# Two graph-attention layers on one core: the same steps in another order on every engine

## The chip, the cores and the metric

The kernel runs on one core of a Trainium2 chip. The metric is the device time of one execution in microseconds (us): the median of three runs before the change is 1123.22 us, the runs lie between 1122.74 and 1124.8. All views below come from one profiled execution of the kernel before.

## The reference

64 graphs of 128 nodes with 384 features pass two attention layers; every layer is followed by a residual and a layer norm. Cut to what is computed:

```python
# layer 0: 6 heads of 64
q, k, v = heads(x @ Wq + bq), heads(x @ Wk + bk), heads(x @ Wv + bv)
probs = softmax(q @ k.T / 8 + where(adj, 0, -9e15))
x1 = layernorm(x + (probs @ v) @ Wf + bf)
# layer 1: 12 heads of 32
h = x1 @ W                                   # per head
src, dst = tanh(h) . w_src, tanh(h) . w_dst
attn = leaky_relu(src + dst.T, 0.2); attn[~adj] = -999; attn = softmax(attn)
feat = elu(attn @ h + b)
gate = sigmoid(x1 @ H_w.T + H_b)
out = layernorm(x1 + gate * feat + (1 - gate) * x1)
```

## The kernel before, in words

The work goes pair by pair: 32 pairs of graphs, and g (0 or 1) is the graph in its pair. Large products are made of three passes in a high and a low part (`product`, L454 to L461): nine matmuls of 384 columns for a 128x384 result, two times nine of 256 columns for the queries and keys of one third j of the heads.

All five engines run one loop over turns (`turns`, L108 to L120). Each engine has its own list of steps, written out by hand at the end of its block, and works it off in this order: an engine that waits in one step does not go on to the next. What a step waits for are counters of other steps (`now` and `prev`, L71 to L75). A step is given the stage of its pair: in turn t, `turn.step(0, ...)` works on pair t, `turn.step(1, ...)` on pair t-1; `turn.late` works one pair further back, so that `late(0, ...)` is on pair t-1 and `late(2, ...)` on pair t-3. The first turns, -1 to 3, and the last ones, 31 to 34, are written out; a step whose pair does not exist is left out in them.

One pair's way, with the names used below (PE is TensorE, DVE VectorE, ACT ScalarE, POOL GpSimd, SP the engine that issues DMAs):

- qk0, qk1, qk2 (PE `queries_keys`, L479): queries and keys in PSUM; ACT copies them as q_hi and k_hi (L721, L722), DVE subtracts to q_lo and k_lo (L964, L967). sc0 and sc1 (`scores`, L545) need all three j of them. v0, v1 are the values.
- DVE adds the mask and takes the minimum, ACT takes the exponent, PE transposes the weights (pt00, pt01, pt10, pt11: graph and half, L567), att0 multiplies them by the values, ct transposes the context, pr projects it, and x1 is normed (`norm0`, ACT L813).
- Layer 1: PE transposes x1 (x1t0, x1t1, L498), h0 and h1 (`hidden`) and the gate's rows g0, g1 multiply it. ACT takes tanh (th), POOL multiplies (prod, L1318), DVE sums (L1008) and splits the sums in three small parts, PE transposes these (sdt, L529), ACT copies them to sd_t (L765), a DMA lays them flat, and PE makes the logits z0, z1 (`attention1`, L613 and L617).
- z goes ACT copy (L793), DVE leak (`z_leak`, L1129), DVE maximum (`z_maxima`, L1136), POOL subtract (`z_subtract`, L1353), ACT exponent (L818). Then a third is transposed by PE (wt0, wt1, L626) and the rest by DMA, out of p_hi (ACT L824) and p_lo (`weights1_low`, POOL L1360). a1, written attend1(g, k), multiplies the weights by h in three parts of 12 matmuls (L640, L642); features, gate, mix, norm1 (ACT L840) and the store follow.

PSUM has two banks for the large products (lin), two for transposes (tp), three joined ones for scores and logits (zp) and one for the two attentions (fp). `LIN_USERS`, `TP_USERS`, `ZP_USERS` and `FP_USERS` (L124 to L127) list who uses them, in PE's order; `SECOND_BANK` says which users take the second bank, and `last_reader` (L140) finds from these lists whose reader PE has to wait for.

## Time and profile before

| | |
|---|---|
| median of three runs | 1123.22 us |
| span of the profiled execution | 1121.2 us, 2.0 below the median |
| PE busy, weight loads | 1047.1 us (93%), 950.8 us (85%) |
| DVE, ACT, POOL busy | 1025.2 (91%), 893.5 (80%), 947.2 us (84%) |
| DMA | 91.33 MB, mean 81 GB/s |
| one turn in the middle | 32.65 us |

The span is cut by the pipeline: the first four turns fill it, turns 4 to 30 repeat the same pattern to a hundredth of a microsecond, and from turn 31 on it drains. PE's matmuls are pipelined, so the start of a row less the start of the row before it is what one matmul costs; the length in a row is longer. A wait of PE can stand on PE or on its weight loads (PEld).

### The profile page before, as it was taken

How to read it: one execution, taken by the hardware profiler on the slowest of the kernel's cores; microseconds unless marked ns; L12 is line 12 of the kernel's file. 1: busy time of each engine (PE TensorE's matmuls, PEld its weight loads, DVE VectorE, ACT ScalarE, POOL GpSimd, SP SyncE). 2: the span in 40 equal slices, each digit the busy share in tenths (PEclk: the TensorE clock that was granted, in tenths of full speed). 3: DMA queues.
4: the chain of work that ended last, by engine and by line, in shares of the span. 5: the costliest groups of instructions: out<-in, count | busy, mean ns of one | idle time of the engine just before them, and what ended most of it. 6: DMA issues, size and time to landing. Idle time of an engine off the chain costs nothing.

```text
span 1121.2 us, 32794 instructions
## 1 busy us (share of the span) xinstructions
PE 1047.1 (93%) x10890; PEld 950.8 (85%) x10890; DVE 1025.2 (91%) x2138; ACT 893.5 (80%) x1739; POOL 947.2 (84%) x781
## 2 busy tenths in 40 slices
PE   4899999999999999999999999999999999999761
PEld 4888889889898988889898888889888888988641
DVE  5589999999999999999999999999999999999854
ACT  4568888888888888888888888888888888888753
POOL 2158889988888998888899888889988888998775
PEclk9899999999999999999999999999999999999975
DMA  6103333232333333234333323433332243332232
GB/s 200 32 21 73 98 84 89 76 86 66 82 97 83 89 79 84 70 79 97 83 89 81 82 74 74 97 83 89 83 82 77 69 97 83 93 81 72 47 67 73
DMA packets 188717, 91.33 MB, mean 81 GB/s; under 512 B 158864, under 2 KB 183696, under 8 KB 188688
## 3 DMA queue, kind: packets, MB, share of 16 engines
q1 hardware_dynamic: 188688, 90.95, 32.7%
q8 instruction: 17, 0.28, 0.1%
q14 instruction: 12, 0.10, 0.0%
HBM read 31.61 MB, written 12.58 MB: 39 GB/s over the span
## 4 chain that ended last, share of the span: by engine, by line
PE 73%; issue 9%; DVE 8%; POOL 4%; ACT 3%; DMA 1%; DVEq 0%; SPq 0%; POOLq 0%; ACTq 0%
PE lin L459 42%; PE zp L554 6%; PE zp L613 3%; PE zp L617 3%; PE fp L583 3%; PE tp L498 3%; PE tp L567 3%; PE tp L626 2%; DVE sd L1008 2%; PE tp L595 2%; PE fp L586 2%; PE fp L640 2%; ACT th L736 1%; ACT sd_t L765 1%; POOL z L1353 1%
## 5 line engine op out<-in xcount | busy, mean ns | idle before, releaser
L1353 POOL TENSOR_TENSOR z<-z,z_max 128x1536 f32<-128x1536 f32 x64 | 176.4, 2757 | 21.3 <-DVE z_max L1136 18.9
L818 ACT ACTIVATE z<-z,log_scale 128x1536 f32<-128x1536 f32 x64 | 101.3, 1583 | 53.7 <-POOL z L1353 53.6
L1360 POOL TENSOR_TENSOR p_lo<-z,p_hi 128x1024 f16<-128x1024 f32 x64 | 137.3, 2145 | 2.3 <-ACT p_hi L824 2.3
L1365 POOL TENSOR_TENSOR f<-f,x_kept 128x384 f32<-128x384 f32 x64 | 65.0, 1016 | 72.0 <-DVE f L1168 72.0
L1318 POOL TENSOR_TENSOR prod<-th,w_sd_rows 128x768 f32<-128x768 f32 x64 | 117.9, 1842 | 6.6 <-ACT th L736 6.4
L784 ACT ACTIVATE p<-p,p_min 128x128 f32<-128x128 f32 x384 | 118.9, 399 | 4.7 <-DVE p_min L1068 4.7
L1129 DVE SCALAR_TENSOR_TENSOR z<-zp,z 128x1536 f32<-128x1536 f32 x64 | 111.9, 1748 | 2.3 <-ACT z L793 2.3
L1136 DVE TENSOR_REDUCE z_max<-z 128x12 f32<-128x1536 f32 x64 | 111.6, 1744 | 0.1
L793 ACT ACTIVATE z<-zp 128x1536 f32<-128x1536 f32 x64 | 93.2, 1457 | 17.8 <-PE zp L617 17.8
L1331 POOL TENSOR_TENSOR v_part<-v_res,v_part 128x384 bf16<-128x384 f32 x64 | 63.0, 984 | 35.8 <-ACT v_part L755 33.8
L459 PE MATMUL lin<-xt_hi,Wq_hi 128*128 128x256 f32 x288 | 81.0, 281 | 12.7 <-DVE Wk_lo L926 12.4
L640 PE MATMUL fp<-h_part,p1t_hi 128*128 128x33 f16 x1536 | 71.9, 178 | 9.5 <-DMA p1t_lo<-p_lo 6.9
L459 PE MATMUL lin<-xt_lo,Wq_hi 128*128 128x256 f32 x288 | 80.5, 280 | 0.0
L459 PE MATMUL lin<-xt_hi,Wq_lo 128*128 128x256 f32 x288 | 80.5, 280 | 0.0
L459 PE MATMUL lin<-xt_hi,Wk_lo 128*128 128x256 f32 x288 | 80.4, 279 | 0.0
L459 PE MATMUL lin<-xt_hi,Wk_hi 128*128 128x256 f32 x288 | 80.4, 279 | 0.0
L459 PE MATMUL lin<-xt_lo,Wk_hi 128*128 128x256 f32 x288 | 80.4, 279 | 0.0
L1378 POOL TENSOR_TENSOR y<-f,x_kept 128x384 f32<-128x384 f32 x64 | 70.3, 1098 | 7.6 <-ACT out_tile L840 7.2
L640 PEld LDWEIGHTS fp<-h_part,p1t_hi 128*128 128x128 f16 x1536 | 63.6, 96 | 14.2 <-DMA p1t_lo<-p_lo 7.3
L1076 DVE SCALAR_TENSOR_TENSOR p0t_lo<-tp,p0t_hi 128x384 f16<-128x384 f32 x128 | 67.1, 545 | 7.5 <-ACT p0t_hi L799 4.5
L459 PE MATMUL lin<-Hw_hi,x1t_hi 128*128 128x384 f32 x192 | 73.8, 384 | 0.0
L459 PE MATMUL lin<-W_hi,x1t_hi 128*128 128x384 f32 x192 | 71.1, 371 | 2.1 <-DVE x1t_lo L975 2.0
(162 smaller groups left out, 4394.2 us busy)
## 6 DMA issues: line engine op xcount, KB each, us to landing
xt_raw<-x_t SPq DMA_DIRECT2D x32, 384.0 KB, 4.0
...
dst_row<-sd_t SPq DMA_DIRECT2D x64, 9.0 KB
p1t_hi<-p_hi SPq DMA_TRANSPOSE x64, 3.2
p1t_lo<-p_lo SPq DMA_TRANSPOSE x64, 3.1
```

Of the source, the lines that this page charges most:

```text
L459: last = pe.matmul(bank, a(k), b(k), start=(opens and k == 0 and i == 0), stop=(k == C - 1 and i == 2))
L554: last = pe.matmul(zp[:, half, N * j:N * (j + 1)], q[p, j, own], k[p, j, own], start=(j == 0 and i == 0), stop=(i == 2), skip_group_check= ...
L640: pe.matmul(o, hi, h_part[i][:, g, h, :], start=(h == 0 and i == 0), stop=False, skip_group_check=True)
L784: last = act.activation(p0[:, g, N * h:N * (h + 1)], p0[:, g, N * h:N * (h + 1)], ACT.Exp, bias=p0_min[:, g, h:h + 1], scale=-1.0)
L793: act.activation(z[:, g, :], zp[:, :, :].rearrange("p b n -> p (b n)"), ACT.Copy)\
L818: act.activation(z[:, g, :], z[:, g, :], ACT.Exp, bias=log_scale[:, :]).then_inc(z_exp[g].sem, 1)
L1129: dve.scalar_tensor_tensor(out=z[:, g, :], in0=zp[:, :, :].rearrange("p b n -> p (b n)"), scalar=0.2, in1=z[:, g, :], op0=ALU.mult, op1=AL ...
L1136: dve.tensor_reduce(z_max[:, g, :], z[:, g, :].rearrange("p (a n) -> p a n", a=H1), AX.X, ALU.max).then_inc(z_maxed[g].sem, 1)
L1318: pool.tensor_tensor(prod[:, g, :].rearrange("p (s d) -> p s d", s=2), th[:, g:g + 1, :].to_broadcast([128, 2, D]), rows["w_sd"][:, :].rea ...
L1353: pool.tensor_tensor(zs, zs, z_max[:, g, :].unsqueeze(2).to_broadcast([128, H1, N]), ALU.subtract)\
L1360: pool.tensor_tensor(p1_lo[:, g, :], z[:, g, PE_HEADS * N:], p1_hi[:, g, :], ALU.subtract).then_inc(w1_lo[g].sem, 1)
L1378: pool.tensor_tensor(y2[:, g, :], f[:, g, :], x1_kept[:, g, :], ALU.add).then_inc(y2_ready[g].sem, 1)
```

## The change

Nothing is computed in another way. Each engine's list has another order; the four lists of PSUM users follow PE's new order, and `SECOND_BANK` becomes a table with other members. A new `later` works two pairs further back, and some steps change from `step` to `late` or from `late` to `later` (or back), which moves them across the border of the turn. Turns -1 to 4 are now written out, and the loop begins at turn 5. On SP two waits that stood together are separated by the loop's spare increment.

```diff
+    def shifted(self, turns, stage, function, *which):
+
+        if self.runs(stage, turns):
+            self.behind = turns
             function(*which)
             self.behind = 0
...
+    def late(self, stage, function, *which):
+        self.shifted(1, stage, function, *which)
+
+    def later(self, stage, function, *which):
+        self.shifted(2, stage, function, *which)
...
-    for t in range(-1, 4):
+    for t in range(-1, 5):
...
-    with eng.Fori(4, PAIRS - 1) as t:
+    with eng.Fori(5, PAIRS - 1) as t:
...
-LIN_USERS = ("h1", "g0", "qk0", "v0", "pr0", "g1", "pr1", "qk1", "qk2", "v1", "h0")
+LIN_USERS = ("qk1", "h0", "qk2", "qk0", "h1", "v0", "v1", "pr0", "g0", "g1", "pr1")
...
-        turns_back += users[i] in LATE_USERS
+        turns_back += LATE_USERS.get(users[i], 0)
...
                     sp.wait_ge(w1_hi[g].sem, now(w1_hi[g]))
+                    turn.apart()
                     sp.wait_ge(f_mm[g].sem, now(f_mm[g]))
...
-                turn.late(0, scores, 1)
+                turn.step(0, scores, 1)
...
-                turn.step(1, hidden, 0)
+                turn.late(1, hidden, 0)
```

PE's turn was x1t1, sc1, a1(0), h1, pt00, pt01, g0, qk0, a1(1) with sdt inside it, pt10, pt11, att0 0, z0, ct0, att0 1, v0, pr0, ct1, z1, g1, pr1, qk1, qk2, wt0, x1t0, v1, sc0, h0, wt1. It is now qk1, h0, att0 0, pt10, qk2, wt0, qk0, pt11, x1t1, a1(0) with sc0 inside it, h1, ct0, wt1, v0, sc1, a1(1) with v1 inside it, pr0, sdt, att0 1, pt00, g0, ct1, z0, g1, pr1, pt01, x1t0, z1.

First place: PE ahead of sc0. Before, from the last matmul of qk2 (lin1) through wt0, x1t0 and the nine matmuls of v1 (lin0) to the first of sc0 (zp); qk_lo0 to qk_lo2 are DVE's counters for q_lo and k_lo:

```order
L459 MATMUL lin1<-xt_hi,Wk_lo 128x256
L626 MATMUL tp1<-ident,z 128x128 [waits ct_lo,z_exp]
L626 MATMUL tp1<-ident,z 128x128 x3
L498 MATMUL tp0<-ident,x1 128x128 [waits pt_lo0,x1_ready]
L498 MATMUL tp0<-ident,x1 128x128 x2
L459 MATMUL lin0<-Wv_hi,xt_hi 128x384 [waits xt_split,qk_lo1]
...
L554 MATMUL zp<-k_hi,q_hi 128x128 [waits qk_lo1,qk_lo2,qk_lo0,z_leaky]
```

Now, from the last matmul of qk0 (lin0) through pt11, x1t1 and twelve matmuls of a1 to sc0:

```order
L470 MATMUL lin0<-xt_hi,Wk_lo 128x256
L578 MATMUL tp1<-ident,p0 128x128 [waits wt_lo,sc_exp]
L578 MATMUL tp1<-ident,p0 128x128 x2
L509 MATMUL tp0<-ident,x1 128x128 [waits pt_lo0,x1_ready]
L509 MATMUL tp0<-ident,x1 128x128 x2
L651 MATMUL fp<-h_part0,p1t_hi 128x33 [waits wt_lo,h_done1,ctx_ready]
...
L565 MATMUL zp<-k_hi,q_hi 128x128 [waits qk_lo1,qk_lo2,qk_lo0,z_leaky]
```

The last product that sc0 needs now stands two times three transposes and twelve small matmuls ahead of it, without a large product in between.

Second place: PE around sdt. Before, in the last part of a1(1); the counters sd_part3 (DVE's small parts) and sd_copied (ACT's sd_t) are those of the same turn:

```order
L642 MATMUL fp<-h_part0,p1t_lo 128x33
L529 MATMUL tp0<-ident_bf,sd_parts 128x128 [waits pt_lo0,sd_part3]
L529 MATMUL tp0<-ident_bf,sd_parts 128x128
L640 MATMUL fp<-h_part0,p1t_hi 128x33
...
L567 MATMUL tp0<-ident,p0 128x128 [waits sd_copied,sc_exp]
L567 MATMUL tp0<-ident,p0 128x128 x2
```

Now, from the last matmul of pr0 (lin1) through sdt and att0 1 (fp from v_part and p0t) to pt00:

```order
L470 MATMUL lin1<-Wf_hi,ctx_lo 128x384
L540 MATMUL tp1<-ident_bf,sd_parts 128x128 [waits wt_lo,sd_part3]
L540 MATMUL tp1<-ident_bf,sd_parts 128x128
L594 MATMUL fp<-v_part0,p0t_hi 128x65 [waits pt_lo0,v_done2,f_norm]
...
L578 MATMUL tp1<-ident,p0 128x128 [waits sd_copied,sc_exp]
L578 MATMUL tp1<-ident,p0 128x128 x2
```

sdt moved behind pr0, and 30 matmuls of att0 instead of 12 of a1 stand between it and the transposes that wait for its reader.

Third place: POOL around the two z_subtract (z, z_max). Before, both stood in the middle of the turn, with a step of the values, the mix, a deviation and the mask between them:

```order
L1353 TENSOR_TENSOR z<-z,z_max 128x1536 [waits z_maxed]
L1330 ISA
L1331 TENSOR_TENSOR v_part2<-v_res,v_part1 128x6x64 [waits v_done1]
L1378 TENSOR_TENSOR y2<-f,x1_kept 128x384 [waits out_ready,x1_copied1,f_gated]
L1343 ISA
L1344 TENSOR_TENSOR rstd<-rstd,half_neg 128x1 [waits y_var]
L1290 REGISTER_ALU
L1294 TENSOR_SCALAR mask0<-adj0 128x256 [waits adj0_loaded,sc_masked]
L1353 TENSOR_TENSOR z<-z,z_max 128x1536 [waits z_maxed]
```

Now graph 0's is the last step of a turn, and graph 1's stands in the next turn between the two `weights1_low` (p1_lo):

```order
L1371 TENSOR_TENSOR p1_lo<-z,p1_hi 128x1024 [waits wt_turned0]
L1364 TENSOR_TENSOR z<-z,z_max 128x1536 [waits z_maxed]
L1326 REGISTER_ALU
L1329 TENSOR_TENSOR prod<-th,w_sd_rows 128x768 [waits sd_sum,h_tanh]
L1309 REGISTER_ALU
L1313 TENSOR_SCALAR mask1<-adj1 128x256 [waits adj1_loaded,z_mm]
L1371 TENSOR_TENSOR p1_lo<-z,p1_hi 128x1024 [waits wt_turned1,w1_hi]
L1329 TENSOR_TENSOR prod<-th,w_sd_rows 128x768 [waits sd_sum,h_tanh]
```

What follows z on every engine moved with it: exponent, p_hi, p_lo, wt, a1, the features, norm1 and the store of a pair are now all in the turn after the one of its z0 and z1. A pair's first step, qk1, is the first of PE's turn t, and its last, norm1 of graph 1, the last of ACT's turn t+3.

## Rows read from the trace of the kernel before

**Rows 1.** Page, busy time of each engine, share of span, instructions

```profile
PE 1047.1 (93%) x10890; PEld 950.8 (85%) x10890; DVE 1025.2 (91%) x2138; ACT 893.5 (80%) x1739; POOL 947.2 (84%) x781
```

**Rows 2.** Windows: stretch, length, busy by engine (instructions), granted clock, DMA share, GB/s

```profile
154.00:1000.00 846.00, 833.88 (x8815) 759.74 (x8814) 814.82 (x1709) 711.91 (x1402) 764.95 (x623) 1.00 0.34 83
1060.00:1080.00 20.00, 11.99 (x106) 10.36 (x104) 13.43 (x32) 11.56 (x16) 15.17 (x12) 0.83 0.43 75
```

**Rows 3.** Timeline of ACT, sd_t in two turns: start, length, engine, line, [idle before]

```profile
491.70 0.38 ACT L765 ACTIVATE sd_t<-tp 128x256 bf16<-128x256 bf16 x1 [0.49 <-issue]
...
524.36 0.38 ACT L765 ACTIVATE sd_t<-tp 128x256 bf16<-128x256 bf16 x1 [0.49 <-issue]
```

**Rows 4.** Timeline of PE and its weight loads where they wait in a turn

```profile
509.19 0.31 PEld L498 LDWEIGHTS tp<-ident,x 128*128 128x128 f32 x3 [0.24 <-ACT x L813]
...
515.00 0.19 PEld L554 LDWEIGHTS zp<-k_hi,q_hi 64*128 64x128 f32 x2 [0.17 <-issue]
...
523.98 0.11 PEld L529 LDWEIGHTS tp<-ident_bf,sd_parts 128*128 128x128 bf16 x2 [0.25 <-DVE sd_parts L1030]
...
524.88 0.85 PE L567 MATMUL tp<-ident,p 128*128 128x128 f32 x6 [0.32 <-ACT sd_t L765]
```

**Rows 5.** Timeline, from a queries-and-keys product to the scores (first turn, later turn)

```profile
22.54 0.28 PE L459 MATMUL lin<-xt_hi,Wk_lo 128*128 128x256 f32 x1
...
22.86 0.47 ACT L721 ACTIVATE q_hi<-lin,bq_col 128x256 fp32r<-128x256 f32 x1
...
23.23 0.47 ACT L722 ACTIVATE k_hi<-lin,bk_col 128x256 fp32r<-128x256 f32 x1
...
25.41 0.47 DVE L967 SCALAR_TENSOR_TENSOR k_lo<-lin,bk_col,k_hi 128x256 fp32r<-128x256 f32 x1
...
26.03 0.33 PE L554 MATMUL zp<-k_hi,q_hi 64*128 64x128 f32 x2 [1.57 <-DVE k_lo L967]
...
509.41 0.46 ACT L722 ACTIVATE k_hi<-lin,bk_col 128x256 fp32r<-128x256 f32 x1
...
509.90 0.48 DVE L964 SCALAR_TENSOR_TENSOR q_lo<-lin,bq_col,q_hi 128x256 fp32r<-128x256 f32 x1
...
510.30 0.48 DVE L967 SCALAR_TENSOR_TENSOR k_lo<-lin,bk_col,k_hi 128x256 fp32r<-128x256 f32 x1
```

**Rows 6.** Timeline of PE: a1 (36 matmuls), h1, six transposes, g0

```profile
516.15 0.22 PE L640 MATMUL fp<-h_part,p1t_hi 128*128 128x33 f16 x2
...
517.07 0.42 PE L459 MATMUL lin<-W_hi,x1t_hi 128*128 128x384 f32 x1
...
518.72 0.82 PE L567 MATMUL tp<-ident,p 128*128 128x128 f32 x6
519.29 0.42 PE L459 MATMUL lin<-Hw_hi,x1t_hi 128*128 128x384 f32 x1
```

**Rows 7.** Timeline of ACT: qk0's q_hi of pairs 0, 1, 4 and 31

```profile
16.59 0.48 ACT L721 ACTIVATE q_hi<-lin,bq_col 128x256 fp32r<-128x256 f32 x1 [3.79 <-PE lin L459]
...
39.93 0.48 ACT L721 ACTIVATE q_hi<-lin,bq_col 128x256 fp32r<-128x256 f32 x1
...
135.86 0.48 ACT L721 ACTIVATE q_hi<-lin,bq_col 128x256 fp32r<-128x256 f32 x1
...
1017.31 0.48 ACT L721 ACTIVATE q_hi<-lin,bq_col 128x256 fp32r<-128x256 f32 x1
```

**Rows 8.** Timeline of POOL: z_subtract of the last pair, graphs 0 and 1

```profile
1089.61 2.75 POOL L1353 TENSOR_TENSOR z<-z,z_max 128x1536 f32<-128x1536 f32 x1 [1.33 <-DVE z_max L1136]
...
1096.82 2.75 POOL L1353 TENSOR_TENSOR z<-z,z_max 128x1536 f32<-128x1536 f32 x1 [3.50 <-DVE z_max L1136]
```

**Rows 9.** Page, DVE's two costliest groups: busy and mean ns of one, idle before, releaser

```profile
L1129 DVE SCALAR_TENSOR_TENSOR z<-zp,z 128x1536 f32<-128x1536 f32 x64 | 111.9, 1748 | 2.3 <-ACT z L793 2.3
L1136 DVE TENSOR_REDUCE z_max<-z 128x12 f32<-128x1536 f32 x64 | 111.6, 1744 | 0.1
```

More of the change, by code:

```diff
@@ L120, in turns @@
         body(Turn(eng, t, passed, counts))
-LIN_USERS = ("h1", "g0", "qk0", "v0", "pr0", "g1", "pr1", "qk1", "qk2", "v1", "h0")
-TP_USERS = ("x1t1", "pt00", "pt01", "sdt", "pt10", "pt11", "ct0", "ct1", "wt0", "x1t0", "wt1")
-ZP_USERS = ("sc1", "z0", "z1", "sc0")
-FP_USERS = ("f0", "f1", "ctx0", "ctx1")
-LATE_USERS = ("h1", "g0", "pr0", "g1", "pr1", "x1t1", "pt00", "pt01", "sdt", "pt10", "pt11", "ct0", "ct1", "sc1", "z0", "z1", "f0", "f1", "ctx0", "ctx1")
-SECOND_BANK = ("g0", "v0", "pr1", "qk2", "h0", "x1t1", "pt01", "pt11", "ct0", "ct1", "wt0")
+LIN_USERS = ("qk1", "h0", "qk2", "qk0", "h1", "v0", "v1", "pr0", "g0", "g1", "pr1")
+TP_USERS = ("pt10", "wt0", "pt11", "x1t1", "ct0", "wt1", "sdt", "pt00", "ct1", "pt01", "x1t0")
+ZP_USERS = ("sc0", "sc1", "z0", "z1")
+FP_USERS = ("ctx0", "f0", "f1", "ctx1")
+LATE_USERS = {"x1t1": 1, "f0": 1, "h1": 1, "g0": 1, "f1": 1, "sdt": 1, "pt10": 1, "pt11": 1, "ctx0": 1, "z0": 1, "ct0": 1, "ctx1": 1, "pr0": 1, "ct1": 1, "z1": 1, "g1": 1, "pr1": 1, "wt0": 1, "h0": 1, "wt1": 1}
+BANKS = {"pt00": 1, "g0": 1, "sdt": 1, "pt11": 1, "v0": 1, "pr0": 1, "pr1": 1, "qk1": 1, "qk2": 1, "wt0": 1, "x1t0": 1, "wt1": 1}
 def bank_of(user):
-    return int(user in SECOND_BANK)
+    return BANKS.get(user, 0)
 def last_reader(turn, users, user, readers):
@@ L644, in attend1 @@
                         last.then_inc(f_mm[g].sem, 1)
+                turn.step(0, queries_keys, 1)
+                turn.late(1, hidden, 0)
+                turn.late(0, attend0, 0)
+                turn.late(0, weights0_transposes, 1, 0)
+                turn.step(0, queries_keys, 2)
+                turn.late(2, weights1_transposes, 0)
+                turn.step(0, queries_keys, 0)
+                turn.late(0, weights0_transposes, 1, 1)
                 turn.late(1, x1_transposes, 1)
-                turn.late(0, scores, 1)
                 turn.late(2, attend1, 0, 0)
+                turn.step(0, scores, 0)
                 turn.late(2, attend1, 0, 1)
@@ L1191, in shift_norm1 @@
                         .then_inc(norm1_shift[g].sem, 1)
-                turn.late(2, features_negative, 1)
+                turn.later(1, gate_raised, 1)
+                turn.late(0, weights0_low, 0, 1)
+                turn.later(0, stats0, 1)
+                turn.later(0, moments0, 1)
+                turn.later(0, variance0, 1)
+                turn.step(0, queries_keys, 1)
+                turn.step(0, later_weight, "W1")
+                turn.later(1, z_leak, 1)
+                turn.later(0, shift_norm0, 1)
@@ L1194, in body @@
+                turn.late(0, context_inverse, 0)
+                turn.late(1, hidden_raised, 0)
+                turn.later(1, z_maxima, 1)
                 turn.late(0, weights0_low, 1, 0)
-                turn.late(0, weights0_low, 1, 1)
-                turn.late(0, context_inverse, 0)
                 turn.late(0, context_norm, 0)
-                turn.late(2, elu, 1)
-                turn.late(1, gate_raised, 0)
+                turn.late(2, turned1_low, 0)
+                turn.step(0, queries_keys, 2)
@@ L1200, in body @@
+                turn.step(0, later_weight, "Hw")
                 turn.step(0, queries_keys, 0)
                 turn.step(0, later_weight, "Wf")
-                turn.late(0, context_inverse, 1)
+                turn.late(0, weights0_low, 1, 1)
+                turn.late(1, x1_low, 1)
+                turn.step(0, scores_masked, 0)
+                turn.late(2, features_inverse, 0)
+                turn.late(1, source_target_sums, 0)
+                turn.step(0, scores_min, 0)
+                turn.late(2, features_norm, 0)
@@ L1240, in body @@
+                turn.late(1, source_target_part2)
+                turn.late(2, features_norm, 1)
+                turn.late(1, source_target_part3)
                 turn.step(0, scores_min, 1)
                 turn.step(0, biases_and_unit)
-                turn.step(1, source_target_sums, 0)
-                turn.step(1, hidden_raised, 1)
+                turn.late(2, features_negative, 1)
+                turn.late(0, add_residual, 0)
+                turn.late(0, context_inverse, 1)
+                turn.late(2, elu, 1)
@@ L1244, in body @@
+                turn.late(0, context_norm, 1)
+                turn.late(2, stats1, 0)
+                turn.late(0, stats0, 0)
+                turn.step(0, value_residue, 1)
+                turn.late(0, moments0, 0)
+                turn.late(2, moments1, 0)
+                turn.late(1, gate_raised, 0)
+                turn.late(0, variance0, 0)
+                turn.late(0, context_low, 1)
+                turn.late(2, variance1, 0)
                 turn.step(0, weights0_low, 0, 0)
+                turn.late(2, stats1, 1)
```

228 lines of the change are left out of this document (94 added, 134 removed).

## The prediction

> **What bounds the kernel now.** I read the page's busy row first, then the windows of the steady stretch, then the timeline of each engine over one turn, and last both ends of the span. The busy row puts PE at 93% and DVE at 91% [rows 1]. In the stretch from 154 to 1000 us PE is busy 833.88 of 846 us and DVE 814.82, at full granted clock [rows 2]. One turn there is 524.36 - 491.70 = 32.66 us, from sd_t to sd_t [rows 3]; over the 27 turns between qk0 of pairs 4 and 31 it is (1017.31 - 135.86) / 27 = 32.65 [rows 7]. The matmuls of one PE step follow each other without a gap: twelve of a1 take a third of 517.07 - 516.15 = 0.92 us, so 0.31, a 384-column product 518.72 - 517.07 = 1.65, three transposes half of 519.29 - 518.72 = 0.57, so 0.285 [rows 6]. What is left to win in the middle is where PE or its weight loads stand still [rows 4]: 0.25 us ahead of sdt, for DVE's small parts; 0.32 ahead of pt10, for ACT's sd_t, since both use one transpose bank; 0.24 ahead of x1t0, for ACT's norm0. Together 0.81 us a turn. I therefore take PE with these three waits as the bound of the middle.
>
> The ends are the other part. qk0 of pair 0 reaches ACT at 16.59 and that of pair 4 at 135.86: the first four turns take 119.27 us, 11.3 less than four full ones. From q_hi of pair 31 at 1017.31 to the end of the span at 1121.2 the drain takes 103.9 us, a little over three full turns [rows 7]: emptier turns gain almost nothing there, since one pair's chain is longer than the work left, and PE's clock falls, to 0.83 granted in the mean of the stretch from 1060 to 1080 [rows 2].
>
> **The change part by part.** No instruction of the computation is added or removed; only orders and waits count. I cost the additional SP increments at nothing: none of the waits in [rows 4] is ended by a DMA.
>
> *Waits that go: -0.81 a turn.* Behind h1 the chain to sdt is tanh, prod, two sums and the small parts. PE now has v0, sc1, v1 and pr0 between h1 and sdt, three products of 1.65 us [rows 6], a scores step and a1(1), where it had one such product, qk0 and two thirds of a1(1); sd_t has the 30 matmuls of att0 1 as cover, about 0.9 us at the pace of a1's 36 in 0.92. x1t0 now stands behind g1, pr1 and pt01, some 3.6 us after z0, and norm0 0 follows the first copy of z on ACT. I give all three back in full. What is late next is below.
>
> *A wait that comes: +1.20 a turn.* sc0 needs q_lo and k_lo of all three j, and the last product before it is now qk0, with only pt11, x1t1 and a third of a1 between: 0.285 + 0.285 + 0.31 = 0.88 us, say 0.9. The chain behind qk0 is read in pieces [rows 5]. From the start of the last matmul to ACT's q_hi: 22.86 - 22.54 = 0.32. From q_hi to the end of k_hi: 23.23 + 0.47 - 22.86 = 0.84. To DVE's q_lo: 509.90 - (509.41 + 0.46) = 0.03. To the end of k_lo: 510.30 + 0.48 - 509.90 = 0.88. To the first matmul of the scores, which reads four waits: 26.03 - (25.41 + 0.47) = 0.15. The sum is 2.22 from the last matmul's start, 2.1 from the start of the next step. PE stands still for 2.1 - 0.9 = 1.2 us, even if ACT and DVE are free at once. Behind the waiting sc0 in PE's queue stand the rest of a1, h1 and everything else of the turn; nobody can be served meanwhile. Today v1, a large product, lies in that gap and there is no such wait.
>
> *Net in the middle.* A scores step already costs PE's weight loads 0.17 of reading its waits [rows 4]; ahead of the new sc0 this lies inside the 1.2. So 1.20 - 0.81 - 0.17 = +0.22 us a turn. Ends: -0.81 if the new wait has a cover that I don't see, +1.2 if the three old waits only move. I take +0.2 (turn 32.85), nearest to the rows, times 27 turns: +5.4 us.
>
> *The first turns: -8.* h0 leaves the second turn for the third, wt leaves the third for the fourth; sc1, pt00 and pt01, which stood at the head of the second turn, ahead of its qk0 at 39.93 [rows 7], now stand at the end of the first, so that border stays. One product and its chain less in the second turn, wt with its copies less in the third: I take 4 us each from the four turns' 119.27. Ends: 0, if the chain of one pair sets these turns as well, and -12.
>
> *The last turns: +18.* Before, the last pair goes from q_hi at 1017.31 to its z_subtract at 1089.61, 72.3 us, and from there to the end in 31.6 [rows 7, 8]. In the new order z_subtract of graph 0 is POOL's last step of the turn that makes z0, for the last pair turn 33. From q_hi of its qk1, about 2.3 us into turn 31 (one product of 18 matmuls ahead of it), there are a full turn 31 and most of turns 32 and 33. These lose their queries, values and scores, but the loop from h1 through prod, sdt, sd_t, the flat DMA, z0 and the copy and leak of z stays, and POOL's two z_subtract and two p_lo stand ahead of the second prod. I put them at 30 us each, an estimate, since the drain before gained nothing at all. z_subtract starts at 32.85 - 2.3 + 30 + 30 = 90.6 us behind q_hi, 18 later than before. Behind it the same work follows as today: the second graph's z_subtract came 7.2 us after the first [rows 8], and now comes as late, since POOL does p_lo of graph 0 first. The 31.6 stay. Ends: +10, if turns 32 and 33 fall to 26, and +24 at full length.
>
> *Sum.* 1121.2 + 5.4 - 8 + 18 = 1136.6 us of span. The profiled span lies 2.0 below the median of the runs, so 1138.6 for the median; I forecast 1137, since the pieces of the ends are rounded upward.
>
> **The rivals.**
>
> *Faster: DVE, not PE, is the bound, and the new order frees it.* In the steady stretch DVE has 814.82 / 846 x 32.65 = 31.45 us of work and 1.2 us idle [rows 2], much of it gaps between small steps that wait for each other; the new list puts other steps between them. Then PE's new wait would lie in room that PE has anyway. If 0.75 of the 1.2 go, the turn is 31.9: 27 x (-0.75) = -20; with the ends (+10) the span is 1111 and the median 1113. Against it: PE is busy 98.6% of the same stretch, and its matmul starts leave no 1.2 us free beyond rows 4. The Trainium skill (Perfetto Trace Analysis, Identifying the Most-Contended Engine) says that matmul busy time is no good measure of PE's headroom and that weight-load busy time is one: by that page PE, at 89.8% of weight loads (759.74 of 846) [rows 2], has room, and DVE is the engine to look at. By that rule this rival would be the forecast; the starts in rows 6 speak against it, since they are not modelled ends. Chance 0.14.
>
> *No change.* The drain runs at its own chain, as it does today, and gains what the fill gains: turns 32 and 33 at 26 us (+10), the fill at -12, the middle even. 1119 to 1123 of span, 1123 in the median. Chance 0.16.
>
> *Slower still: a second loop takes over.* From qk1's q_lo to qk0's q_lo DVE has the leak and the maximum of z of graph 1, 1.75 + 1.74 us [rows 9], two pairs of q_lo and k_lo at 0.88 [rows 5] and four steps of about half a microsecond, together some 7.3 us; PE's h0, att0 0, pt10, qk2, wt0 and qk0 leave it, by my estimate, 7.5. The second copy of z on ACT stands ahead of qk1's q_hi. If ACT or DVE come later than that by more than 0.2 us, sc0 waits longer by all of the excess, each turn. At 0.5 us more: 27 x 0.7 + 10 = +29, span 1150, median 1152. Chance 0.15.
>
> **How the numbers follow.** The forecast has 0.55, its own range is 1128 to 1146 (middle -0.1 to +0.4 a turn, the ends +5 to +15). The range to 1118 below takes in the even case and a little of the faster one; to 1156 above the second loop. Faster by over 0.2% (below 1121.0, about what three runs can tell): 0.16, the first rival and some of the second. Within 0.2%, to 1125.5: 0.14. Slower: 0.70.
>
> **What would show it.** Right: in the steady part PE waits ahead of sc0 (the scores' line) for DVE's k_lo, about 1.2 us each turn, the waits ahead of sdt, pt10 and x1t0 are gone, the turn is 32.7 to 33.1; q_hi of the last pair's qk1 lies some 120 us ahead of the end. Wrong: a turn below 32.4, no wait at sc0, or another engine's wait there that is longer; a drain of less than 112 us from that q_hi; or a clock that falls in the middle of the span.

## The result and the profile after

The changed kernel takes 1193.8 us in the median of four runs (1192.71 to 1194.97), the kernel before 1123.7 us on the same chip; the ratio of the runs is 1.063, 95% interval 1.061 to 1.064. The forecast was 1137 us with a range to 1156: the direction is right, the size far off. The profiled span is 1190.7 us, 69.5 more than before.

The page's busy row of the kernel after, as [rows 1]; VectorE's busy time has grown by 65.3 us, with the same 2138 instructions:

```profile
PE 1053.0 (88%) x10890; PEld 953.8 (80%) x10890; DVE 1090.5 (92%) x2138; ACT 898.3 (75%) x1739; POOL 944.1 (79%) x781
```

The windows of the kernel after, the stretch of [rows 2] and one of the drain:

```profile
154.00:1000.00 846.00, 792.40 (x8319) 719.80 (x8317) 822.67 (x1626) 679.86 (x1328) 723.35 (x591) 1.00 0.32 79
...
1130.00:1150.00 20.00, 8.25 (x94) 6.91 (x93) 13.25 (x20) 10.89 (x16) 16.22 (x13) 0.61 0.30 59
```

VectorE is busy 97% of the steady stretch; TensorE, at full clock, fell from 98.6% to 93.7%. The chain of work that ended last, followed back by the page, lay 73% on PE and 8% on DVE before; now it lies 41% on DVE and 9% on PE. One turn, from ScalarE's sd_t to sd_t as in [rows 3], takes 34.42 us instead of 32.66:

```profile
497.64 0.38 ACT L776 ACTIVATE sd_t<-tp 128x256 bf16<-128x256 bf16 x1 [1.26 <-issue]
...
532.06 0.38 ACT L776 ACTIVATE sd_t<-tp 128x256 bf16<-128x256 bf16 x1 [1.25 <-issue]
```

Where the time went is read from ScalarE's q_hi of the first product of a turn (qk1 now, qk0 in [rows 7]), pairs 0, 4 and 31:

```profile
15.41 0.47 ACT L732 ACTIVATE q_hi<-lin,bq_col 128x256 fp32r<-128x256 f32 x1 [4.44 <-PE lin L470]
...
131.08 0.47 ACT L732 ACTIVATE q_hi<-lin,bq_col 128x256 fp32r<-128x256 f32 x1
...
1060.88 0.47 ACT L732 ACTIVATE q_hi<-lin,bq_col 128x256 fp32r<-128x256 f32 x1
```

The start is 1.2 us earlier; the first four turns take 115.7 us (-3.6); the 27 turns of the middle (1060.88 - 131.08) / 27 = 34.44 us each, +48.3 in all; the drain 1190.7 - 1060.88 = 129.8 us (+25.9). The sum is 69.4. So 70% of the loss lies in the middle.

The groups by line name the instructions that became longer (busy us, mean ns of one | idle before). Before:

```profile
L1163 DVE TENSOR_SCALAR f_neg<-f 128x384 f32<-128x384 f32 x64 | 23.4, 366 | 3.8
L1030 DVE TENSOR_TENSOR sd_parts<-sd_res,sd_parts 128x48 bf16<-128x48 f32 x32 | 6.7, 208 | 3.3
L1021 DVE TENSOR_TENSOR sd_res<-sd,sd_parts 128x48 f32<-128x48 f32 x32 | 6.7, 208 | 3.3
L1026 DVE CAST sd_parts<-sd_res 128x48 bf16<-128x48 f32 x32 | 6.0, 189 | 3.3
```

After:

```profile
L1174 DVE TENSOR_SCALAR f_neg<-f 128x384 f32<-128x384 f32 x64 | 70.3, 1098 | 0.1
L1037 DVE CAST sd_parts<-sd_res 128x48 bf16<-128x48 f32 x32 | 23.2, 726 | 0.1
L1041 DVE TENSOR_TENSOR sd_parts<-sd_res,sd_parts 128x48 bf16<-128x48 f32 x32 | 16.9, 527 | 0.1
L1032 DVE TENSOR_TENSOR sd_res<-sd,sd_parts 128x48 f32<-128x48 f32 x32 | 12.8, 401 | 0.2
```

The clamp f_neg and three of the four small steps have gained 80 us between them; the other large groups of VectorE are within 4% of what they were (z_leak 1748 ns in both, as in [rows 9]). VectorE's busy time grew by less, 65.3 us, because it counts once what two rows share: a row now overlaps the next by some 0.08 us, and the small steps stood apart before. One turn of VectorE's timeline, kernel after, shows when they are long:

```profile
517.87 0.48 DVE L975 SCALAR_TENSOR_TENSOR q_lo<-lin,bq_col,q_hi 128x256 fp32r<-128x256 f32 x1
518.27 0.47 DVE L978 SCALAR_TENSOR_TENSOR k_lo<-lin,bk_col,k_hi 128x256 fp32r<-128x256 f32 x1
...
523.84 1.89 DVE L1174 TENSOR_SCALAR f_neg<-f 128x384 f32<-128x384 f32 x1
525.65 0.68 DVE L1153 TENSOR_TENSOR p1t_lo<-tp,p1t_hi 128x512 f16<-128x512 f32 x1
...
529.47 0.36 DVE L1032 TENSOR_TENSOR sd_res<-sd,sd_parts 128x48 f32<-128x48 f32 x1
...
529.93 0.73 DVE L1037 CAST sd_parts<-sd_res 128x48 bf16<-128x48 f32 x1
...
531.10 0.53 DVE L1041 TENSOR_TENSOR sd_parts<-sd_res,sd_parts 128x48 bf16<-128x48 f32 x1
```

GpSimd's timeline of the same turn:

```profile
523.69 1.82 POOL L1329 TENSOR_TENSOR prod<-th,w_sd_rows 128x768 f32<-128x768 f32 x1
525.47 1.95 POOL L1321 TENSOR_TENSOR x_raw<-x_raw,bf_rows 128x768 f32<-128x768 f32 x1
528.74 1.02 POOL L1376 TENSOR_TENSOR f<-f,x_kept 128x384 f32<-128x384 f32 x1 [1.32 <-DVE f L1179]
529.71 0.91 POOL L1342 TENSOR_TENSOR v_part<-v_res,v_part 128x384 bf16<-128x384 f32 x1
530.57 1.00 POOL L1381 TENSOR_TENSOR f<-f,gate 128x384 f32<-128x384 f32 x1
```

Each long row ends just behind the GpSimd row beside it: f_neg at 525.73, prod at 525.51; the subtraction sd_res at 529.83, the difference f<-f,x_kept at 529.76; the cast at 530.66, v_part at 530.62; the last small step at 531.63, the gating f<-f,gate at 531.57. All four read and write SBUF only; p1t_lo, which reads PSUM, keeps its 0.68 us beside raise_x. In the kernel before, the same steps lay in a stretch in which GpSimd waited for elu 0. VectorE there:

```profile
489.88 0.35 DVE L1163 TENSOR_SCALAR f_neg<-f 128x384 f32<-128x384 f32 x1
490.17 0.19 DVE L1017 CAST sd_parts<-sd 128x48 bf16<-128x48 f32 x1
490.46 0.21 DVE L1021 TENSOR_TENSOR sd_res<-sd,sd_parts 128x48 f32<-128x48 f32 x1
490.77 0.19 DVE L1026 CAST sd_parts<-sd_res 128x48 bf16<-128x48 f32 x1
491.06 0.21 DVE L1030 TENSOR_TENSOR sd_parts<-sd_res,sd_parts 128x48 bf16<-128x48 f32 x1
```

and GpSimd, whose idle time of 2.21 us covers all of them:

```profile
491.90 1.01 POOL L1365 TENSOR_TENSOR f<-f,x_kept 128x384 f32<-128x384 f32 x1 [2.21 <-DVE f L1168]
```

This is the theory that the experiments test first: a VectorE step whose operands all lie in SBUF stands still until the GpSimd instruction beside it ends. The Trainium skill (SBUF — State Buffer, Who interferes with whom) states it more narrowly: VectorE's second pair of SBUF ports is GpSimd's only pair, an exclusive lock for a whole instruction, which copies, casts, tensor_scalar and steps with two SBUF inputs can need. The rows above agree. Not every step in SBUF alone stands still: the reduction p_min, begun at 531.56 and soon beside the mix of GpSimd (531.65), takes its usual 0.94 us.

TensorE's timeline of the same turn, where it stands still, as [rows 4]:

```profile
517.23 0.52 PE L578 MATMUL tp<-ident,p 128*128 128x128 f32 x3 [0.27 <-DVE p1t_lo L1153]
...
518.85 0.33 PE L565 MATMUL zp<-k_hi,q_hi 64*128 64x128 f32 x2 [0.48 <-issue]
...
526.47 0.20 PE L651 MATMUL fp<-h_part,p1t_hi 128*128 128x33 f16 x2 [0.57 <-DVE p1t_lo L1153]
...
531.69 0.28 PE L540 MATMUL tp<-ident_bf,sd_parts 128*128 128x128 bf16 x2 [0.81 <-DVE sd_parts L1041]
```

The two longest waits are behind stretched steps: p1t_lo of graph 1 is queued behind the long clamp, sdt waits for the last small step. The 0.48 us ahead of sc0, the wait that the prediction had named, is the rival cause in the runs below.

### The profile page after: what moved, and what is told of

Its sections match the earlier page's. It is cut to its first block, busy times and chain, and to the rows that moved or that the text cites. A ratio compares the mean times of both kernels' runs of the same rounds, so it can differ in the third digit from the quotient of the medians.

```text
span 1190.7 us, 32961 instructions
## 1 busy us (share of the span) xinstructions
PE 1053.0 (88%) x10890; PEld 953.8 (80%) x10890; DVE 1090.5 (92%) x2138; ACT 898.3 (75%) x1739; POOL 944.1 (79%) x781
## 4 chain that ended last, share of the span: by engine, by line
DVE 41%; issue 27%; ACT 13%; PE 9%; POOL 7%; DMA 1%; DVEq 1%; ACTq 1%; POOLq 0%; SPq 0%
DVE p_min L1079 4%; ACT p L795 4%; DVE z_max L1147 4%; DVE z L1140 3%; PE zp L565 3%; DVE p1t_lo L1153 3%; DVE sd L1019 3%; DVE ctx_n L1099 3%; ACT out_tile L851 3%; PE lin L470 3%; DVE ctx_lo L1106 2%; DVE stats L1184 2%; DVE p L1070 2%; ACT z L804 2%; DVE h_res L1004 2%
## 5 line engine op out<-in xcount | busy, mean ns | idle before, releaser
L1376 POOL TENSOR_TENSOR f<-f,x_kept 128x384 f32<-128x384 f32 x64 | 65.3, 1021 | 90.3 <-DVE f L1179 90.3
L1140 DVE SCALAR_TENSOR_TENSOR z<-zp,z 128x1536 f32<-128x1536 f32 x64 | 111.9, 1748 | 2.5 <-ACT z L804 2.5
L470 PE MATMUL lin<-xt_hi,Wq_hi 128*128 128x256 f32 x288 | 92.5, 321 | 16.3 <-DVE Wk_lo L937 11.6
L651 PE MATMUL fp<-h_part,p1t_hi 128*128 128x33 f16 x1536 | 75.8, 179 | 32.6 <-DVE p1t_lo L1153 20.7
L651 PEld LDWEIGHTS fp<-h_part,p1t_hi 128*128 128x128 f16 x1536 | 66.7, 97 | 45.6 <-issue 29.7
L845 ACT ACTIVATE f_neg<-f_neg 128x384 f32<-128x384 f32 x64 | 33.5, 523 | 73.0 <-DVE f_neg L1174 73.0
L1347 POOL TENSOR_TENSOR xt_lo<-xt_raw,xt_hi 128x768 fp32r<-128x768 f32 x32 | 58.9, 1839 | 21.2 <-ACT xt_hi L861 21.2
L565 PE MATMUL zp<-k_hi,q_hi 64*128 64x128 f32 x384 | 57.9, 287 | 19.9 <-issue 18.0
L578 PE MATMUL tp<-ident,p 128*128 128x128 f32 x384 | 65.6, 280 | 10.1 <-DVE p1t_lo L1153 9.9
```

What stands on the lines that cost most here:

```text
L470: last = pe.matmul(bank, a(k), b(k), start=(opens and k == 0 and i == 0), stop=(k == C - 1 and i == 2))
L565: last = pe.matmul(zp[:, half, N * j:N * (j + 1)], q[p, j, own], k[p, j, own], start=(j == 0 and i == 0), stop=(i == 2), skip_group_check= ...
L578: last = pe.transpose(bank[:, N * i:N * (i + 1)], p0[:, g, c:c + N], ident[:, :])
L651: pe.matmul(o, hi, h_part[i][:, g, h, :], start=(h == 0 and i == 0), stop=False, skip_group_check=True)
L1140: dve.scalar_tensor_tensor(out=z[:, g, :], in0=zp[:, :, :].rearrange("p b n -> p (b n)"), scalar=0.2, in1=z[:, g, :], op0=ALU.mult, op1=AL ...
```

## The experiments

Turn: mean of the 24 turns between the sixth and the thirtieth sd_t of the profile. DVE: the page's busy time. Ratio: to runs of the kernel before on the same chip, with its interval. Turn and DVE are of the profiled run. In the kernel after the last of the 24 turns takes 35.4 us and the others 34.44. The profiled run of f2 took 1145.4 us, the longest of its four; that of e4 took 1278.4, and the time given for e4 is that of its three others.

| kernel | us | ratio | turn | DVE |
|---|---|---|---|---|
| before | 1123.7 | | 32.65 | 1025.2 |
| after | 1193.8 | 1.063 [1.061, 1.064] | 34.48 | 1090.5 |
| e1, after: clamps from PSUM | 1191.6 | 1.061 [1.059, 1.063] | 34.41 | 1066.2 |
| f1, after: clamp 0 from PSUM | 1167.9 | 1.041 [1.039, 1.042] | 33.59 | 1063.3 |
| e2, after: reordered | 1202.2 | 1.070 [1.068, 1.072] | 34.70 | 1055.2 |
| e4, after: scores 0 later | 1260.5 | 1.119 [1.113, 1.126] | 37.44 | 1088.4 |
| f2, after: short GpSimd steps | 1141.1 | 1.016 [1.015, 1.018] | 32.71 | 1025.2 |
| k2, after: clamps on ScalarE | 1164.8 | 1.039 [1.037, 1.040] | 33.59 | 1041.6 |
| e3, before: raise_x beside | 1178.6 | 1.049 [1.048, 1.051] | 34.43 | 1076.3 |
| e3s, the same, raise_x short | 1123.9 | 1.002 [1.001, 1.003] | 32.76 | 1028.7 |
| f3, before: short GpSimd steps | 1124.8 | 1.002 [1.001, 1.003] | 32.76 | 1027.7 |
| h1, before: loop a turn later | 1124.8 | 1.002 [1.001, 1.003] | 32.74 | 1027.3 |
| g1, before: clamp between parts | 1126.5 | 1.005 [1.003, 1.006] | 32.83 | 1023.7 |
| g2, before: two banks exchanged | 1121.2 | 0.999 [0.998, 1.000] | 32.64 | 1025.2 |
| g3, before: banks and norm0 | 1129.9 | 1.007 [1.005, 1.008] | 32.96 | 1022.8 |
| k1, before: clamps on ScalarE | 1134.2 | 1.011 [1.009, 1.012] | 33.05 | 1012.8 |
| k3, before: clamp 0 twice | 1130.4 | 1.007 [1.006, 1.009] | 32.89 | 1032.7 |

### e3: the collision made in the kernel before

```diff
 # GpSimd
-                turn.late(0, raise_x)
...
+                turn.step(0, raise_x)
                 turn.step(2, features_difference, 0)
```

> The kernel before, with one step moved on GpSimd alone: raise_x (1.85 us, 128x768) goes from behind mix 0 to just ahead of features_difference 0, into the 2.2 us in which GpSimd waited for elu 0 while VectorE did the clamp and the four small steps. No step depends on the other, and raise_x would end at about 491.6 us of the profiled turn, before features_difference 0 began (491.9). The collision theory expects the clamp of graph 0 to be stretched from 0.35 to about 1.7 us, the steps behind it to be late by as much, and the turn to grow from 32.65 by 1.0 to 1.6 us: 1155 to 1170 us. Without such a collision the rows keep their 0.35 and 0.2 us and the time stays within 0.3% of 1123.7 us.

Measured 1178.6 us. VectorE's timeline, then GpSimd's:

```profile
512.13 1.94 DVE L1163 TENSOR_SCALAR f_neg<-f 128x384 f32<-128x384 f32 x1
```

```profile
512.02 1.83 POOL L1310 TENSOR_TENSOR x_raw<-x_raw,bf_rows 128x768 f32<-128x768 f32 x1
```

The clamp, begun 0.11 us behind raise_x, goes from 0.35 to 1.94 us and ends 0.22 us behind it; most turns are 34.20 us, 1.55 longer, and all 55 us of the loss are bought by one step moved on another engine. The time is 9 us above the expected range, although the turn lies inside it. Four turns of the middle took 35.4 or 35.7 us, which makes some 5 of the 9; the rest was not looked into.

### e3s: the same order, a short instruction

```diff
-                    pool.tensor_tensor(x_raw[:, :, :], x_raw[:, :, :],
+                    pool.tensor_tensor(x_raw[:, :, 0:48], x_raw[:, :, 0:48],
...
```

> The kernel before with raise_x moved beside the clamp as in the run that took 1178.6 us, but raising only 48 of its 384 columns per graph; the rest of that work is left out. Order and waits are those of that run. The collision theory expects the clamp's stretch to end with the shorter GpSimd instruction: the clamp at 0.35 to 0.6 us instead of 1.9, and most of the 55 us gone, 1120 to 1135 us. If the moved step's place or its waits were the cause, whatever its length, the time stays above 1165 us.

Measured 1123.9 us. VectorE, then GpSimd:

```profile
521.65 0.49 DVE L1163 TENSOR_SCALAR f_neg<-f 128x384 f32<-128x384 f32 x1
```

```profile
521.52 0.40 POOL L1310 TENSOR_TENSOR x_raw<-x_raw,bf_rows 128x96 f32<-128x96 f32 x1
```

The clamp again ends 0.22 us behind the GpSimd row, now at 0.49 us, and the 55 us are gone. It is the length of the instruction beside it, not the order or a wait.

### f2 and f3: the collision taken out of the kernel after, and a control

```diff
 # GpSimd: raise_x, f_diff 0, gated 0, prod 1 on 48 columns, value_part3 1 on one head; as one of them:
-                    pool.tensor_tensor(f[:, g, :], f[:, g, :], x1_kept[:, g, :], ALU.subtract)
+                    n = D if g == 1 else 48
+                    pool.tensor_tensor(f[:, g, 0:n], f[:, g, 0:n], x1_kept[:, g, 0:n], ALU.subtract)
...
```

> The kernel after, in which GpSimd does only a part of the columns in five steps: raise_x, source_target_products 1 and features_difference 0 and gated_features 0 on 48 columns instead of 384, value_part3 1 on one head of six. That part of the work is left out; orders, waits and the other engines' instructions are unchanged. The collision theory expects all of VectorE's stretch to go (2.6 us a turn), the turn to fall by the 1.8 us it had gained and perhaps a little more, until TensorE bounds it: 32.3 to 32.9 us, 1130 to 1148 us. Theories that put the loss on TensorE's order (the wait ahead of the scores) or on the fill and the drain expect less than a third of the 70 us back: 1170 us or more.

> The control: the kernel before with the same five GpSimd steps on the same part of their columns, the rest of that work left out. There VectorE's clamp and small steps lie where GpSimd waits, so the collision theory expects nothing to come back: 1118 to 1126 us. If shorter GpSimd steps help in any order, for example because they free their own consumers earlier, it would gain tens of us here too.

Measured 1141.1 and 1124.8 us. The page's busy row of f2:

```profile
PE 1048.4 (92%) x10890; PEld 957.0 (84%) x10890; DVE 1025.2 (90%) x2138; ACT 904.0 (79%) x1739; POOL 787.3 (69%) x783
```

VectorE's busy time is 1025.2 us, what it was before the change [rows 1], and the turn 32.71. 52.7 of the 70 us are gone, and the same shortening brings nothing in the old order. The rival cause does not fit: TensorE's wait ahead of sc0 is still there in f2, with most of the loss gone:

```profile
503.62 0.33 PE L565 MATMUL zp<-k_hi,q_hi 64*128 64x128 f32 x2 [0.52 <-issue]
```

By f2 the collision therefore costs about 53 us, and about 17 us of the loss do not hang on it. The size rests on this one edit, which also makes GpSimd's own results ready earlier; f3 shows that this brings nothing in the old order, and no run shows it for the new one alone. f1 and k2 below leave GpSimd's work as it was, and clamps alone, one in f1 and both in k2, bring back some 26 and 29 us.

### e1 and f1: the clamp read from PSUM

```diff
-                    dve.tensor_scalar(f_neg[:, g, :], f[:, g, :], 0.0, None, ALU.min).then_inc(f_min[g].sem, 1)
+                    dve.scalar_tensor_tensor(out=f_neg[:, g, :].rearrange("p (a e) -> p a e", a=H1), in0=s[:, :, 0:E1],
+                                             scalar=0.0, in1=f_rcp[:, g, :].unsqueeze(2).to_broadcast([128, H1, E1]),
+                                             op0=ALU.min, op1=ALU.mult).then_inc(f_min[g].sem, 1)
...
```

> The kernel after, with one step made in another form: the clamp of the features (f_neg, 128x384, VectorE) reads the PSUM bank and the reciprocal instead of the tile f in SBUF, and the exponent behind it takes the scale that is left out. Nothing is moved. The collision theory (a step of VectorE whose operands all lie in SBUF stands still until the GpSimd instruction beside it ends) expects graph 0's clamp to fall from 1.89 us to about 0.6 us (the row of the normalisation, the same shape from PSUM, is 0.61), graph 1's to go from 0.45 to 0.6, so VectorE gains 1.1 us a turn, the turn falls from 34.4 to about 33.3 us and the time from 1194 to about 1160 us. The theory that the wait ahead of the scores of graph 0 on TensorE sets the turn expects the same time within 0.3%, 1190 to 1197 us, whatever the clamp's row says.

> The kernel after, with the clamp of graph 0 alone read from PSUM; graph 1's stays as it was, so that the bank of the features is free again after the normalisation of graph 1. (In the first form the bank was held until graph 1's clamp, and attend0 1 waited 1.0 us a turn for it.) The collision theory expects the 1.9 us clamp at 0.6 us, about 0.3 us back from elu 0 that now lies beside raise_x, and the turn about 1.0 us shorter: 33.4 us, 1160 to 1167 us. If VectorE's stretched steps are not what sets the turn, the time stays at 1190 us or above.

s is the PSUM bank of the features, and the clamp is now the last to read it. In e1 graph 0's clamp took 0.54 us, about as expected, yet the time was 1191.6, what the rival had expected: now the clamp of graph 1 held the bank. TensorE's timeline of e1:

```profile
531.59 0.27 PE L594 MATMUL fp<-v_part,p0t_hi 128*128 128x65 bf16 x3 [1.04 <-DVE f_neg L1175]
```

The edit had traded one wait for another, so e1 alone decides nothing. f1, with graph 1's clamp as it was, gives 1167.9 us, 1 us above the expected range, and a turn of 33.59, -0.89. The clamp keeps its time beside prod, which runs from 515.44 to 517.29 there; elu 0, which reads two tiles in SBUF and took 0.54 us, now lies beside raise_x (517.24 to 519.08):

```profile
515.64 0.55 DVE L1178 SCALAR_TENSOR_TENSOR f_neg<-fp,f_rcp 128x384 f32<-128x384 f32 x1
...
518.59 0.91 DVE L1185 SCALAR_TENSOR_TENSOR f<-f_neg,f 128x384 f32<-128x384 f32 x1
```

### k2: the clamp on ScalarE

```diff
-                    act.activation(f_neg[:, g, :], f_neg[:, g, :], ACT.Exp).then_inc(f_exp[g].sem, 1)
+                    act.activation(f_neg[:, g, :], f[:, g, :], ACT.Relu, scale=-1.0).then_inc(f_min[g].sem, 1)
+                    act.wait_ge(f_min[g].sem, now(f_min[g]))
+                    act.activation(f_neg[:, g, :], f_neg[:, g, :], ACT.Exp, scale=-1.0).then_inc(f_exp[g].sem, 1)
...
```

> The kernel after with the clamp on ScalarE in the same way. The collision theory with VectorE as the bound expects VectorE to lose the whole of the two clamps (1.89 + 0.45 us a turn), of which about 0.3 us comes back as a stretch of elu 0 and the small steps stay stretched (1.1 us): the turn about 2 us shorter, 32.4 to 32.8 us, 1125 to 1145 us. If the stretched clamp only stood in a wait that was there anyway, the time stays above 1165 us.

Measured 1164.8 us, turn 33.59: about half the expected gain, and just at the 1165 us that the other reading had named, so taken alone it does not decide. VectorE lost 48.9 us of busy time; elu 0 took 1.10 us beside raise_x, and VectorE now waits 0.30 us a turn ahead of value_residue and 0.33 ahead of elu 1 for ScalarE.

### e2: the order repaired, in part

```diff
 # VectorE, behind value_residue 0
+                turn.step(0, scores_masked, 1)
                 turn.late(1, source_target_sums, 1)
+                turn.late(2, features_negative, 0)
 ... source_target_part1, _residue, _part2, _part3
                 turn.late(2, elu, 0)
                 turn.late(2, features_inverse, 1)
                 turn.late(2, features_norm, 1)
...
```

> The kernel after, with the same instructions and only their order changed: on GpSimd raise_x goes ahead of weights1_low 1; on VectorE the clamp of graph 0 and the four small steps of source_target go, in one run, behind the sums of graph 1, where GpSimd has nothing to do until elu 0; the masking of graph 1's scores goes ahead of these sums; ScalarE's exponent of the clamp goes behind the exponents of the scores. The collision theory expects the clamp at 0.35 us and the four small steps at 0.2 us each again, 2.5 us a turn less VectorE time; some 0.5 us of it comes back as waits between the small steps, so the turn is about 32.5 us and the time about 1135 us. The theory of the wait ahead of the scores on TensorE expects no change, 1190 to 1197 us, since neither the scores' chain nor TensorE's order is touched.

Measured 1202.2 us. The clamp was 0.35 and the small steps 0.2 us again, and VectorE's busy time fell by 35 us, but the time rose by 8 us, where 1135 us were expected. In the order I wrote TensorE waited 1.0 us a turn ahead of attend0 1, which needs normalisation 1 and value_part3 1, and elu 1 fell beside mix 0 of GpSimd (1.26 us). A failed repair: it shows that VectorE's busy time alone does not make the turn, and decides nothing on the cause.

### e4: scores 0 later

```diff
 # TensorE
-                turn.step(0, scores, 0)
                 turn.late(2, attend1, 0, 1)
                 turn.late(2, attend1, 0, 2)
+                turn.step(0, scores, 0)
...
```

> The kernel after, with scores 0 on TensorE behind all three thirds of attend1 0 instead of behind the first, and on VectorE the masking of these scores behind features_inverse 0 and the sums of graph 0. The theory of the wait ahead of the scores expects the 0.5 us of wait there to go and the turn to fall by about that: 33.9 us, 1178 us. The collision theory expects the clamp of graph 0 still at 1.5 us or more, the wait to show up elsewhere, and the turn within 0.2 us of 34.4: 1188 to 1199 us.

Measured 1260.5 us (1247.8 to 1262.7), against both theories. In the profile, of a run of 1278.4 us, the second third of attend1 stands still for its transposed weights now that the scores do not stand in between, and then the clock falls. The mean granted clock was 0.90 in this run, 0.92 to 0.94 in the other three and 0.97 in the kernel after. TensorE's wait, and the windows:

```profile
519.56 0.22 PE L651 MATMUL fp<-h_part,p1t_hi 128*128 128x33 f16 x2 [1.71 <-DMA p1t_lo<-p_lo]
```

```profile
515.00:520.00 5.00, 3.03 (x48) 2.75 (x48) 4.15 (x10) 4.76 (x10) 5.00 (x3) 0.98 0.81 174
520.00:525.00 5.00, 5.00 (x40) 4.85 (x37) 3.47 (x5) 1.38 (x2) 2.59 (x3) 0.50 0.38 74
```

TensorE was busy 3.03 of 5 us, and the next 5 ran at 0.50 of full speed (1.2 GHz). In the kernel after the scores were cover for that transfer; the run does not isolate the wait ahead of them.

### g1, g2, g3, h1: the kernel before, one thing at a time

```diff
 # g1, VectorE
                 turn.step(1, source_target_part1)
+                turn.step(2, features_negative, 0)
                 turn.step(1, source_target_residue)
+                turn.late(2, shift_norm1, 1)
 # g2 (and g3)
-SECOND_BANK = ("g0", "v0", "pr1", "qk2", "h0", "x1t1", "pt01", "pt11", "ct0", "ct1", "wt0")
+SECOND_BANK = ("g0", "v0", "pr1", "qk2", "h0", "x1t1", "pt01", "pt10", "ct0", "ct1", "wt0")
 # h1
-    for t in range(-1, 4):
+    for t in range(-1, 5):
```

> The kernel before, with the clamp of graph 0 moved on VectorE behind source_target_part1 and the shift of the output's graph 1 moved behind source_target_residue, so that both fill the 0.1 us in which each small step waits for the one before it, and the parts end earlier. TensorE waited 0.25 us a turn for the last part. The collision theory (all of them still lie in GpSimd's gap) expects rows at 0.35 and 0.2 us, that wait gone or nearly so, and 0.1 to 0.25 us a turn less: 1116 to 1121 us. If the wait for the parts is covered by the next one (sd_t, 0.32 us a turn), the time is within 0.2% of 1123.5.

> The kernel before with one entry of the PSUM list: the transposes pt10 use the second bank and pt11 the first, instead of the other way round, so that pt10 no longer waits for ScalarE's copy sd_t to free the bank of the transposes before it (0.32 us a turn on TensorE). pt11 takes that wait over, but starts 0.4 us later by itself. If TensorE's waits set the turn of the kernel before, as the prediction has it, the turn falls by about 0.3 us: 1112 to 1116 us. If another chain (VectorE's steps behind the parts) sets it, nothing: 1120 to 1125 us.

> The kernel before with the banks of pt10 and pt11 exchanged, and the chain to the normalised x of graph 0 moved forward: on GpSimd deviation0 0 goes ahead of mix 1, on VectorE shift_norm0 0 ahead of stats1 0, on ScalarE norm0 0 ahead of weights1_high 0. TensorE waited 0.24 us a turn for that x ahead of the transposes x1t0. If TensorE's waits set the turn, both go: 0.5 us a turn, 1104 to 1110 us. If not, 1118 to 1126 us.

> The kernel before with one part of the change alone: the loop begins one turn later, so one more turn is written out ahead of it; orders and banks are those of before. If the written-out turn costs time of its own (the border theory), it shows here: 1126 us or more. The forecast counted it at nothing: within 0.2% of 1122.4, 1120 to 1125 us.

g2 takes away the largest of the three waits that the prediction called the bound, and gains at most 0.2%: the turn is 32.64 us. The wait has come back 0.7 us later. Weight loads of g2:

```profile
491.41 0.31 PEld L567 LDWEIGHTS tp<-ident,p 128*128 128x128 f32 x3 [0.15 <-issue]
492.10 0.15 PEld L583 LDWEIGHTS fp<-v_part,p0t_hi 128*128 128x128 f16 x3 [0.38 <-DVE f L1154]
```

g3, which also moves the chain of norm0, is slower by 7.5 us: with ScalarE's norm0 ahead, VectorE waits 0.45 us a turn for k_hi. g1 is slower by 4, where a gain was expected: the first small step now waits 0.2 us for the sums, and the last one 0.2 us for the step before it. h1 costs 0.2%, the edge of what can be told, and its turn is 0.1 us longer although it leaves every order as it was; f3 and e3s show as much. What makes this tenth is open, and no cause is read from a tenth of a microsecond a turn here.

### k1 and k3: work taken off VectorE and put on it

```diff
 # k3, VectorE (k1 has the edit of k2 in the kernel before)
+                    if g == 0:
+                        dve.tensor_scalar(f_neg[:, 1, :], f[:, 0, :], 0.0, None, ALU.min)
                     dve.tensor_scalar(f_neg[:, g, :], f[:, g, :], 0.0, None, ALU.min).then_inc(f_min[g].sem, 1)
```

> The kernel before with the clamp taken off VectorE: ScalarE makes it as a rectified linear step of the negated features just ahead of its exponent (which takes the scale -1). VectorE has 2 x 0.36 us a turn less, ScalarE 2 x 0.5 us more. If VectorE sets the turn of the kernel before, the turn falls by 0.5 to 0.75 us, to about 32.0: 1098 to 1108 us, below both kernels. If TensorE with its three waits sets it, as the prediction has it, only the wait for the small parts (0.25 us) can go, and the exchange of banks has shown that such a wait comes back elsewhere: 1115 to 1124 us.

> The kernel before with the clamp of graph 0 done twice on VectorE (the first time into the other graph's half of f_neg, which is free then): about 0.29 us more VectorE work a turn, in the stretch in which GpSimd waits, and nothing else. If VectorE sets the turn, 0.25 to 0.4 us a turn come on top: 1130 to 1136 us. If TensorE's waits set it and VectorE has 1.2 us of room a turn, the time stays within 0.3% of 1122.4.

k3: 1130.4 us; the second clamp starts 0.27 us behind the first, and the turn is 0.24 longer. So VectorE has no room at that place, although it idles 1.2 us a turn. k1: 1134.2 us, outside both expected ranges, 1098 to 1108 and 1115 to 1124. VectorE's waits of k1 in the middle (us in total, times, longest):

```profile
DVE p0t_lo L1079 <- ACT p0t_hi L799: 13.4, 23, 0.6
DVE q_lo L967 <- ACT k_hi L722: 7.8, 23, 0.3
```

These waits are 0.58 and 0.34 us a turn, which the kernel before does not show in the middle: ScalarE, with 0.5 us more to do ahead of p0t_hi and of k_hi, is late for VectorE by more than the 0.39 us of busy time a turn that VectorE saved. So in this order what is put on VectorE there is paid in full, but what is handed to ScalarE is not gained.

## Why the prediction was wrong

*The step that failed* is the first sentence of the change part by part: "No instruction of the computation is added or removed; only orders and waits count." It takes the durations of the old trace into the new order. Orders decide what runs beside what, and five rows a turn are longer for it; the sum had no term for that and no bound. The missing term is about 53 us by f2, of the 57 between the forecast and the result; e3 and e3s show the mechanism alone. f2, without it, came to 1141.1, four above the forecast, but that nearness is in part luck: in f2's profile the 27 turns of the middle cost 2 us where the forecast has 5.4, and the ends 20 where it has 10.

*"PE with these three waits as the bound of the middle."* Not borne out. [Rows 4] show the three waits rightly (they leave out two of the weight loads, 0.33 and 0.41 us at 494.46 and 495.20, which cost TensorE's own rows at most 0.1), but a wait that ends in another engine's step is a sign of a loop that passes through both. g2 removed 0.32 us of them for nothing, k3 paid 0.24 us for 0.27 on VectorE. Which engine bounds a turn if VectorE is relieved and ScalarE not loaded was not tried.

*Waits that go, -0.81.* Those of pt10 and x1t0 are gone. That of sdt went from 0.25 to 0.81 us; in f2 it is 0.15, so this too was the collision. The 0.9 us for the 30 matmuls of att0 1 do not follow from a1's pace, which gives 0.77; their own rows before, 495.58 to 496.49, give 0.91.

*A wait that comes, +1.20.* The chain behind qk0 is 518.85 less the end of qk0's steps at 516.81, 2.04 us, against 2.1 predicted [rows 5]. Counted by starts, as the prediction counts, TensorE stands still for about 1.0 of the 1.2 us: 0.42 ahead of pt11 (517.23 less 516.81, of which 0.27 is booked as a wait for p1t_lo of VectorE, a wait that the prediction did not have) and 0.6 ahead of sc0 (0.48 booked). Here the size is off, and one wait is another's.

*Net +0.22 a turn.* Measured +1.79; without the collision +0.06 (f2, 32.71 against 32.65), less than the tenth that h1 leaves open.

*First turns -8, last turns +18.* Measured -3.6 and +25.9. The last z_subtract of graph 0 was to start 90.6 us behind q_hi and starts at 99.9, the end was to follow 31.6 later and follows after 30.0. GpSimd's timeline of the last pair, as [rows 8]:

```profile
1160.74 2.75 POOL L1364 TENSOR_TENSOR z<-z,z_max 128x1536 f32<-128x1536 f32 x1 [3.70 <-DVE z_max L1147]
```

The term that was mis-sized is mainly the 30 us for each of turns 32 and 33: from z_subtract to z_subtract they take 33.1 and 33.3. The stretch ahead of them, 32.85 - 2.3, takes 33.5 instead of 30.55. In f2 the drain is 125.8 and the fill 118.5 us, so the ends of the new order cost some 20 us there too, with the collision gone; that is nearly all that keeps f2 above the kernel before. What makes turns 32 and 33 as long as they are was not tried.

*The rivals.* The first named VectorE as the engine to look at, and the result agrees with that half: VectorE has the largest share, 41%, of the chain that ended last. By the Trainium skill (Perfetto Trace Analysis, Identifying the Most-Contended Engine) the engine of highest occupancy is the one to look at, with TensorE judged by its weight loads; the page of the kernel after, with 92% for VectorE and 80% for the weight loads, agrees. VectorE's idle time did shrink, from 1.20 to 0.95 us a turn (846 - 814.82 and 846 - 822.67, per turn). But it held VectorE's work constant, and that grew from 31.45 to 33.49 us. The second, no change, had an even middle and short last turns; neither came. The third, a second loop of q_lo and k_lo, does not show: VectorE takes up qk0's q_lo at 517.87, 0.03 us behind ScalarE's k_hi.
